# The tail of a two-layer transformer kernel on one core: four engines' orders laid out anew

## What is computed

```python
x = x + attn(ln(x))      # 16 heads of 64, segments of 64 plus every 4th position within 256
x = x + ffn4(ln(x))      # FP4: gate, up (352 wide), silu(gate)*up, down, blocks of 16 quantised
x = x + mixer(ln(x))     # rms norm, q k v a g projections, scan over chunks of 64, gate,
                         # out projection, rms norm, silu MLP of 512
x = x + rwkv(ln(x))      # sigmoid(xr @ Wr) * (relu(xk @ Wk)^2 @ Wv), xr, xk mix x with x shifted by one
```

## Time and profile before

| | us |
|---|---|
| three runs, median | 478.84 |
| lowest, highest | 476.29, 480.12 |
| the profiled execution | 475.18 |
| its span (first to last instruction) | 473.2 |
| TensorE busy in the span | 446.8 |

### The profile page before, as it was taken

The page is one execution under the profiler, slowest core; times in us unless marked ns, Lnnn a source line. Parts: engine busy times, 40 slices in busy tenths (PEclk is TensorE's granted clock), DMA queues, the critical chain, the costliest instruction groups (busy, mean ns, idle before and its releaser), DMA issues.

```text
span 473.2 us, 17264 instructions
## 1 busy us (share of the span) xinstructions
PE 446.8 (94%) x6440; PEld 350.3 (74%) x6440; DVE 395.1 (83%) x1344; ACT 332.3 (70%) x975; POOL 293.8 (62%) x491
## 2 busy tenths in 40 slices
PE   6899979999999999999999999999978889989995
PEld 5677768888888888788888888878644746558674
DVE  5987858888898899889899878987889988998674
ACT  3487747877877877886887786875655588986433
POOL 4234537677666858667867766737588896572122
PEclk9999989999999999999999999999999999999999
DMA  7369682346444444344456554443000000000002
GB/s 222 143 189 246 165 275 52 72 89 129 86 79 105 82 79 104 74 87 92 103 131 134 119 116 85 101 95 71 3 0 0 1 1 1 1 1 1 1 0 90
DMA packets 136098, 40.53 MB, mean 86 GB/s; under 512 B 104976, under 2 KB 131024, under 8 KB 136016
## 3 DMA queue, kind: packets, MB, share of 16 engines
q1 hardware_dynamic: 135440, 38.38, 35.3%
q10 hardware_dynamic: 576, 1.05, 0.7%
HBM read 29.44 MB, written 9.96 MB: 83 GB/s over the span
## 4 chain that ended last, share of the span: by engine, by line
PE 75%; POOL 8%; DVE 7%; ACT 3%; DMA 2%; issue 2%; SPq 1%; ACTq 0%; DVEq 0%; POOLq 0%
PE psum L423 13%; PE psum L465 12%; PE psum L485 7%; PE psum L499 6%; PE psum L1188 6%; PE psum L511 6%; PE psum L496 5%; PE psum L404 4%; PE psum L406 3%; PE psum L405 3%; PE psum L1183 3%; PE psum L1179 2%; POOL area L1834 2%; POOL rs L1879 1%; DMA arena<-in_L_attn_w_q_dram 1%
## 5 line engine op out<-in xcount | busy, mean ns | idle before, releaser
L949 POOL TENSOR_SCALAR pband<-pband,fac 128x192 f32<-128x192 f32 x256 | 103.9, 425 | 85.9 <-DVE fac L771 84.1
L569 ACT ACTIVATE pband<-pband,st 128x192 f32<-128x192 f32 x256 | 113.2, 448 | 0.2 <-DVE st L719 0.2
L719 DVE CUSTOM_DVE_ANT_0 pband<-psum,band_mask 128x192 f32<-128x192 f32 x256 | 76.0, 353 | 1.0 <-PE psum L423 0.9
L423 PE MATMUL psum<-keys,q_class 64*64 64x192 f32 (+2 forms) x1536 | 66.2, 275 | 0.0
L465 PEld LDWEIGHTS psum<-ident,pband 128*128 128x128 f32 x384 | 45.3, 141 | 21.2 <-issue 12.6
L423 PEld LDWEIGHTS psum<-keys,q_class 64*64 64x64 f32 x1536 | 57.4, 133 | 2.8 <-issue 2.0
L465 PE MATMUL psum<-ident,pband 128*128 128x128 f32 x384 | 53.3, 274 | 2.4 <-DVE pt L780 2.4
L569 ACT ACTIVATION_READ_ACCUMULATOR pband<-pband,st 128x1 f32 x256 | 49.5, 193 | 0.0
L931 POOL COPY keys<-k_rows 128x512 f32<-128x512 f32 x32 | 36.1, 1127 | 17.2 <-issue 8.7
L780 DVE COPY pt<-psum 128x512 f32<-128x512 f32 x64 | 43.7, 683 | 3.0 <-PE psum L465 2.4
L939 POOL COPY q_class<-q_rows 128x512 f32<-128x512 f32 x32 | 36.1, 1129 | 11.1 <-ACT q_rows L609 11.1
(11 more groups left out here) (213 smaller groups left out, 1086.4 us busy)
## 6 DMA issues: line engine op xcount, KB each, us to landing
v_rows_dram<-arena SPq DMA_DIRECT2D x32, 256.0 KB, 3.2
v_both<-v_rows_dram SPq DMA_DIRECT2D x32, 256.0 KB, 3.7
v_seg<-v_rows_dram SPq DMA_DIRECT2D x64, 128.0 KB, 3.4
v_side<-v_rows_dram SPq DMA_DIRECT2D x96, 64.0 KB, 2.6
w_rows_dram<-st SPq DMA_DIRECT2D x64, 8.0 KB, 2.9
st<-w_rows_dram SPq DMA_DIRECT2D x64, 8.0 KB, 2.4
arena<-_attn_hidden_states_dram SPq DMA_DIRECT2D x4, 256.0 KB, 4.2
out_dram<-x SPq DMA_DIRECT2D x4, 256.0 KB, 2.5
```

What stands on the lines that cost most here:

```text
L423: return pe.matmul(bank[2 * r + head][rows, at:at + y.shape[1]], x, y, start=True, stop=True, skip_group_check=True)
L569: act.activation(x, x, ACT.Exp, bias=mine[:, head:head + 1], scale=-1.0, accum_out=mine[:, 2 + head:3 + head]).then_inc(s_exp, 1)
L719: dve.tensor_tensor_reduce(pband[:, G % P_SLOTS, c, head, :], bank[2 * r + head][:, at:at + BAND], band_mask[:, (0, 1, 1, 2)[w], SEG * (1 ...
L949: pool.tensor_scalar(x, x, fac[:, F % 2, 1, c, head:head + 1], 1.0, ALU.mult, ALU.mult).then_inc(s_scaled, 1)
```

## The change

The same steps, each on the engine where it was, stand in another order in the lists of TensorE, ScalarE, VectorE and GpSimd, and `STEPS` says so. SyncE's list and all helper functions are unchanged. From the middle of the file on each line number is one smaller in the new file. Cut to the parts that are spoken of below:

```diff
@@ -543,19 +543,20 @@
-            weigh(28, 2); weigh(28, 3); turn(29, 1); turn(29, 0); output(28); turn_weights(0); turn_weights(1); t1(0)
-            turn(29, 3); turn_weights(2); turn(29, 2); weigh(29, 0); weigh(29, 1); turn_weights(3); turn_weights(4)
-            turn_weights(5); turn_weights(6); turn(30, 0); weigh(29, 2); weigh(29, 3); turn(30, 1); turn(30, 2)
-            turn_weights(7); output(29); turn(30, 3); weigh(30, 0); weigh(30, 1); t1(1); weigh(30, 2); weigh(30, 3)
-            turn(31, 0); turn(31, 1); output(30); turn(31, 3); turn(31, 2); weigh(31, 0); t2(0); weigh(31, 1); t1(2)
-            gu0(0); weigh(31, 2); weigh(31, 3); output(31); gu1(0); t1(3); t2(1); gu2(0); gu0(1); gu1(1); gu3(0)
-            gu2(1); t2(2); gu0(2); gu3(1); gu1(2); t2(3); gu2(2); gu0(3); gu3(2); gu1(3); t3a(0); t3b(0); gu2(3)
-            dn(0); t3a(1); gu3(3); t3b(1); dn(1); t4(0); pv(0); pk(0); pg(0); pa(0); pq(0); t3a(2); qq(0); t3b(2)
-            t4(1); dn(2); t3a(3); pk(1); t3b(3); pv(1); dn(3); pa(1); pg(1); t4(2); trx(0); pq(1); pk(2); pv(2); qq(1)
...
+            weigh(28, 2); weigh(28, 3); turn(29, 1); turn(29, 0); output(28); turn_weights(0); turn(29, 3)
+            turn_weights(1); turn_weights(2); t1(0); turn_weights(3); turn(29, 2); turn_weights(4); weigh(29, 0)
+            weigh(29, 1); turn_weights(5); turn_weights(6); turn_weights(7); turn(30, 0); weigh(29, 2); weigh(29, 3)
+            turn(30, 1); turn(30, 2); output(29); turn(30, 3); weigh(30, 0); weigh(30, 1); t1(1); weigh(30, 2)
+            weigh(30, 3); turn(31, 0); turn(31, 1); output(30); turn(31, 3); t2(0); turn(31, 2); weigh(31, 0); gu0(0)
+            t1(2); weigh(31, 1); weigh(31, 2); weigh(31, 3); gu1(0); output(31); t2(1); t1(3); gu2(0); gu0(1); gu3(0)
+            gu1(1); t2(2); gu2(1); gu0(2); gu1(2); t2(3); gu3(1); gu0(3); gu2(2); t3a(0); gu1(3); t3b(0); gu3(2)
+            dn(0); gu2(3); t3a(1); t3b(1); gu3(3); dn(1); t4(0); pv(0); pk(0); t3a(2); pg(0); t3b(2); pa(0); pq(0)
+            t4(1); dn(2); qq(0); t3a(3); pv(1); t3b(3); pk(1); pg(1); dn(3); pa(1); t4(2); pq(1); trx(0); qq(1)
+            pv(2); pk(2); pg(2); t4(3); op(0); trx(1); pv(3); pa(2); pk(3); pq(2); pg(3); pa(3); op(1); qq(2); pq(3)
...
@@ -680,19 +681,19 @@
-            take_out(28); odd_turned(29, 1); band_exps(31, 1); exp_difference(30); take_weights(0); take_weights(1)
-            odd_turned(29, 3); take_weights(2); take_weights(3); take_weights(4); z0(0); take_out(29)
-            odd_turned(30, 1); take_weights(5); exp_difference(31); take_weights(6); take_weights(7)
-            odd_turned(30, 3); qx6(0); take_out(30); odd_turned(31, 1); odd_turned(31, 3); z0(1); silu0(0)
...
+            take_out(28); odd_turned(29, 1); band_exps(31, 1); take_weights(0); exp_difference(30); take_weights(1)
+            take_weights(2); take_weights(3); take_weights(4); odd_turned(29, 3); take_weights(5); take_weights(6)
+            z0(0); take_weights(7); take_out(29); odd_turned(30, 1); exp_difference(31); qx6(0); odd_turned(30, 3)
+            take_out(30); odd_turned(31, 1); odd_turned(31, 3); z0(1); silu0(0); qx6(1); take_out(31); silu1(0)
...
@@ -899,25 +900,24 @@
...
-            bn0(1); qx7(0); ag0(1); even_turned(31, 0); qx8(0); xq(0); even_turned(31, 2); accumulate(30); xqt(0)
-            qx0(1); x1(2); qx2(1); bn0(2); ag0(2); hm0(0); qx7(1); accumulate(31); qx8(1); qx0(2)
-            x1(3); hm1(0); qx2(2); bn0(3); ag0(3); qa0(0); hm2(0); hm0(1); qa2(0); qx7(2); qx8(2); qx0(3)
-            hm1(1); qa0(1); qx2(3); hm3(0); qb0(0); hm2(1); qb2(0); qa2(1); qx7(3); hm0(2); qx8(3)
-            qa7(0); hm3(1); qb0(1); hm1(2); qa8(0); qb2(1); qb7(0); hm2(2); qb8(0); hm0(3); qa0(2)
-            qa7(1); qa2(2); qa8(1); hm1(3); qb7(1); hm3(2); qb8(1); qb0(2); qa0(3); hm2(3); qb2(2); x2(0)
-            bn1(0); ag1(0); qa2(3); hm3(3); qb0(3); qa7(2); qa8(2); qb7(2); qb2(3); x2(1)
-            qb8(2); bn1(1); ag1(1); qa7(3); a1(0); qa8(3); h1(1); qb7(3); qb8(3); aa(0); hqb(3); rq(0)
-            x2(2); bn1(2); e1(0); p(0); ag1(2); f(0); w(0); s(0); x2(3); bn1(3); ag1(3); a1(1); aa(1); qn(0); m(0)
-            w(1); v(2); p(1); h1t(3); rq(1); e1(1); x3_(0); f(1); w(2); qn(1); s(1); m(1); a1(2); y(1); aa(2); h2(0)
-            a1(3); x3_(1); h2t(0); rq(2); aa(3); e1(2); p(2); rq(3); f(2); qn(2); s(2); m(2); e1(3); qn(3); p(3)
...
+            even_turned(30, 2); qx7(0); x1(1); qx8(0); bn0(1); ag0(1); even_turned(31, 0); xq(0); xqt(0)
+            even_turned(31, 2); accumulate(30); qx0(1); qx2(1); x1(2); hm0(0); bn0(2); ag0(2); qx7(1); qx8(1); hm1(0)
+            accumulate(31); qa0(0); qx0(2); x1(3); qx2(2); bn0(3); hm2(0); ag0(3); qa2(0); qx7(2); hm0(1); qx8(2)
+            hm3(0); qb0(0); qx0(3); hm1(1); qx2(3); qb2(0); qa0(1); qa7(0); qx7(3); qx8(3); hm0(2); hm2(1); qa8(0)
+            qa2(1); qb7(0); hm1(2); qb8(0); hm3(1); qb0(1); hm0(3); qb2(1); qa7(1); qa0(2); hm2(2); qa8(1); hm1(3)
+            qb7(1); qa2(2); qb8(1); hm3(2); qa0(3); qb0(2); x2(0); qb2(2); bn1(0); hm2(3); ag1(0); qa7(2); qa2(3)
+            qa8(2); qb7(2); hm3(3); qb8(2); x2(1); qb0(3); bn1(1); ag1(1); qb2(3); qa7(3); h1(1); qa8(3); qb7(3)
+            qb8(3); a1(0); hqb(3); aa(0); w(0); x2(2); bn1(2); ag1(2); rq(0); p(0); e1(0); f(0); s(0); w(1); x2(3)
+            bn1(3); a1(1); ag1(3); qn(0); aa(1); m(0); v(2); rq(1); p(1); h1t(3); e1(1); f(1); qn(1); x3_(0); s(1)
...
@@ -1008,12 +1008,11 @@
-            rs0(1); qx1(1); qx4(1); rs0(2); xq(1); qx1(2); qx4(2); rs0(3); qa1(0); shift_weights(); 
-            qa4(0); qx1(3); xq(2); qa1(1); qx4(3); qb1(0); qb4(0); xq(3); qa4(1); qb1(1)
-            hqa(0); qb4(1); hqb(0); qa1(2); hqa(1); qa4(2); hqb(1); qb1(2); qa1(3); qb4(2)
-            rs1(0); qa4(3); rz1(0); qb1(3); hqa(2); qb4(3); hqb(2); rs1(1); rz1(1); hqa(3); rx(0); u(0)
...
+            rs0(1); qx1(1); qx4(1); shift_weights(); rs0(2); xq(1); qa1(0); qx1(2); qx4(2); rs0(3); qa4(0); xq(2)
+            qx1(3); qb1(0); qx4(3); qb4(0); xq(3); qa1(1); hqa(0); qa4(1); hqb(0); qb1(1); qb4(1); qa1(2); hqa(1)
+            qa4(2); hqb(1); qb1(2); qa1(3); qb4(2); rs1(0); hqa(2); qa4(3); hqb(2); qb1(3); rs1(1); qb4(3); rz1(0)
+            hqa(3); rz1(1); u(0); rs1(2); rx(0); u(1); rs1(3); y(0); rx(1); rz1(3); u(2); rs3(0); rz1(2); rx(2)
...
@@ -1021,36 +1020,36 @@
-        "t1 t2 gu0 gu1 gu2 gu3 t3a t3b dn t4 pv pk pg pa pq qq trx op t5 fc0 fc1 fc2 fc3 pr t6 k r kv",
+        "t1 t2 gu0 gu1 gu2 gu3 t3a t3b dn t4 pv pk pg pa pq qq trx op t5 fc1 fc0 fc3 fc2 pr t6 k r kv",
...
```

62 lines of the change are left out of this document (31 added, 31 removed), and 24 rows, old and new, of the table STEPS.

## The result

The changed kernel took 471.78 us (median of 4 runs, 470.72 to 472.09) beside 477.56 for the kernel before; the ratio of the runs is 0.987, 95% interval 0.984 to 0.991. Run again among the experiments, on another chip, it took 474.09 us (7 runs, 470.69 to 475.74) beside 477.62: 0.992, 0.988 to 0.995. So it is faster, by 1.3% in the one measurement and by 0.8% in the other: 472.1 us over its eleven runs, against 476.9 to 477.6 for before beside it and beside the experiments. The forecast was 475.8 us, 0.6% less than before: right in sign, too small by half against the first measurement. Both medians lie in its range; the first is faster by over 1%, which had a chance of 27%, the second within 1%, which had 69%.

A forecast was written before the change was run, and what follows sets the result against it. TensorE, busy 94% of the span, and its holes (13.1 us idle in the tail) set the time. Gains 0.4 + 1.2 + 0.3 + 0.5 + 1.5 = 3.9, less 0.9, give 3.0 us: 475.8 us, range 471.5 to 480.5.

The forecast's parts named there:

- the last 45 us: From 423.2 us TensorE never stops: no wait becomes real there, and a microsecond won earlier moves the end by one.
- C: Rival, slower: TensorE's queue is held at t3a(2) waiting for hqb(2), 2.4 us lost; 481.3 us, chance 9%.
- 318 to 329.4: Tail stretch in us: factors(31) and its accumulation come earlier, shrinking t1(1)'s wait of 0.55; gain 0.4 us.
- 329.4 to 353.6: Tail stretch: output(31)'s hole closes, gu1(1)'s shrinks, t2(1)'s grows to 1.3; gain 1.2 us.
- 353.6 to 369.7: Tail stretch: four old holes go, new waits of 1.2 at gu1(2) and 1.3 at t2(2); gain 0.3 us.
- 369.7 to 379.7: Tail stretch: waits before dn(1) and t4(0) go, a new 0.6 before t3b(1); gain 0.5 us.
- rival B: The VectorE and GpSimd chain swallows the gain, TensorE merely waiting longer at later steps; 478.3 us, chance 22%.
- 379.7 to 401: Tail stretch: t3a(2) fills the 0.72 wait for v(0), t4(2)'s 1.17 goes, 1.3 stays; gain 1.5 us.
- 401 to 423.2: Tail stretch: old waits of 2.15 us replaced by new ones at t4(3), qq(3) and trx(3); gain 0.
- behind it there is only the last output's two VectorE steps and the store, the same before and after: After 468.2 us, the end of TensorE's work: 5.0 us, taken as unchanged.
- I charge 0.9: Deduction of 0.9 us for VectorE operations on two SBUF tiles meeting GpSimd multiplications and blocking each other.
- rival A: Leads are kept and VectorE-GpSimd meetings get fewer: 3.9 + half of 3.4 = 5.6 us, 473.2 us; chance 27%.

The follow-up runs named there:

- h2: The changed kernel's four lists up to 370 us, the lists of the kernel before behind that: 478.39 us, ratio to before 1.003.
- e1: The changed kernel with VectorE's differences(31) put back behind qx1(0), where it stood before: 471.95 us, ratio to before 0.988.
- e5: The changed kernel with e1's edit and qa0(1) moved behind qa7(0) on VectorE: 472.04 us, ratio to before 0.989.
- e6: The changed kernel with e1's edit, gu3(1) put ahead of gu1(2) on TensorE, hm2(1) and silu3(1) moved earlier: 471.69 us, ratio to before 0.989.
- e4: The changed kernel with t3a(2) back behind pq(0), t3b(2) behind t4(1), and their ScalarE copies later: 476.09 us, ratio to before 0.997.
- b2: The kernel before with b1's edits and z2(0) moved behind ht2(2) on ScalarE: 481.6 us, ratio to before 1.010.
- h3: The lists of the kernel before up to 401 us, the changed kernel's behind that: 475.04 us, ratio to before 0.995.
- e2: The changed kernel up to 451.6 us, the last orders of the kernel before behind that: 475.37 us, ratio to before 0.992.
- b1: The kernel before with only the changed kernel's GpSimd piece, and qb8(2) behind qb7(2) on VectorE: 488.8 us, ratio to before 1.025.
- h1: The lists of the kernel before up to steps begun by 369.7 us, the changed kernel's behind: 472.01 us, ratio to before 0.989.
- e3: The changed kernel with GpSimd's piece put back as before, qa4(3), rz1(0), qb1(3) ahead of hqa(2): 478.24 us, ratio to before 0.999.

## Why the prediction was right and wrong

**Right.** The sign; that no hole appears in the last 45 us and that a lead is passed on (3.7 us at op(2), 3.5 at the end); that output(31) and v(0) no longer hold TensorE; the waits at t2(2), t3b(1) and pv(0), to 0.1 us; that C would not come: hqb(2) ended at 381.36, 1.1 us ahead of pk(0)'s end, where I had it 1 us ahead.

**Wrong: "318 to 329.4 ... Gain 0.4", "329.4 to 353.6 ... gain 1.2", "353.6 to 369.7 ... gain 0.3", "369.7 to 379.7 ... gain 0.5".** 2.4 us in all, and pv(0) came at the same time (0.1 us later). h2 shows it without the rest: this half of the change is worth nothing. The step that failed first is 318 to 329.4: I followed exp_difference(31) and factors(31) and not differences(31), which the change moves ahead of qx0(0) and where VectorE then stands 2.55 us for a DMA. The gain of 0.4 became a loss of 0.5 in the first profile and of 0.1 in the middle one of seven; e1, e5 and e6 put the price of the step at about 0.7. The second is gu1(2), sized 1.2 and measured at 2.78. I took silu, product and hand-overs, as if VectorE were free; but hm0(2) stands behind qa7(0), met by qb4(0) (2.11 us), qx7(3) and qx8(3). The third is t4(0): its wait for h1(0) did not go but grew from 0.46 to 0.67 us. The holes I closed came back at the next step that needs the chain: rival B's reasoning, true for this half.

**Wrong in size: "379.7 to 401 ... gain 1.5".** This is the term that was furthest off for what it gained: 3.4 us, from pv(0) to t4(2). The "about 0.5 behind t3a(3)" that I had set against it did not come, so that of the old 2.82 us of idle time only pv(0)'s 0.78 stayed: 2.0. The other 1.3 us the idle times don't show; part of them is that work begun behind a wait reads longer, the rest I have not split. And the reason beside it, "filled by t3a(2)", was wrong (e4, b2): ScalarE's z2(0) went out of the way, and I had not looked at ScalarE's list there.

**Off by little: "401 to 423.2 ... Gain 0".** The lead of 3.2 us at t4(2) is 3.7 at op(2) and 3.5 at the end, 0.3 more. I had put new waits of 0.95 at t4(3) and 0.6 each at qq(3) and trx(3) against the old 2.15; they were 0.51, 0.25 and none, with 0.25 before qq(1) that I didn't have. h3, which has these orders alone, is 0.6 us ahead at op(2) and 0.4 at the end.

**Wrong: "behind it there is only the last output's two VectorE steps and the store, the same before and after".** The stores of other groups share the end. 0.9 us: 6.98 to 7.01 against 6.08 to 6.14 in all profiles (e2).

**Wrong in sign: "I charge 0.9" for meetings.** They fell by 1.9 us where I charged for more; rival A had "half of 3.4" = 1.7. How much of that reached TensorE can't be told apart: b1 and b2 had the long ones gone as well and won nothing.

Together, by the profiles: -0.14 + 3.36 + 0.29 + 0.89 = 4.4 us (up to pv(0), to t4(2), to TensorE's end, behind it), where I had 2.4 + 1.5 + 0 + 0 less 0.9 = 3.0. The terms up to pv(0) were 2.5 too high and those behind it 3.0 too low. That these two nearly cancel is luck; what is left of the miss is them and the 0.9 charged for meetings. The outcome is nearest to rival A's, the leads kept and fewer meetings, though not by its way; its 473.2 us lies between the two measurements' 471.8 and 474.1.

Open: why the first comparison gives 5.8 us and the tails 4.4. The profile of before was one of its quicker executions (475.18 us, median 477.4 over 75), and the two measurements of the changed kernel differ by 2.3 us, at mean clocks of 0.9955 and 0.9921; I can't do better than 0.8 to 1.3%. Open too is each engine's share. No kernel I ran beats the changed one by more than the measurement can tell (h1, e1, e5 and e6 took 471.7 to 472.0).

## What to carry to other kernels

When a hand-written order of several engines is changed, follow for each moved step what it waits for, DMAs included, and what stands behind it on its own engine; the steps that decided here (differences(31), z2(0), rz1(0)) were small ones on engines that I had looked at only for the big ones. A hole closed on TensorE alone, ahead of a saturated chain, came back here at the chain's next delivery (h2); where VectorE was ahead too, the lead was kept (e1). And what a step behind a DMA costs is seen only over several profiles. Count what leaves at the end, all stores of it, not the last alone.

## What the runs showed of the hardware

A long wait of TensorE may cost twice: behind the wait of 2.2 to 2.8 us before gu1(2) the granted clock fell to 0.5, from 2.4 to 1.2 GHz, for 3.4 us or twice that in six profiles of nine, 1.7 us of clock for each 3.4, and in none of seven without that wait. That they hang together is likely, not proven: six of these seven have the old order there, and e6 alone changed the wait and little else. It fell elsewhere too behind two shorter waits in a row, 0.88 and 0.78 us (h1, at 381.5) and 0.83 and 0.98 (e4, at 393.1), and in one of 2.21 and one of 3.37 us (e3, at 333.5 and 391.5); behind the pair before t4(0) and pv(0), which all sixteen profiles have, only in h1.

The long waits of one order came out the same in every profile (t2(1) 1.79 to 1.80 us, gu1(2) 2.77 to 2.78), but for those on a DMA (t1(1), 0.61 to 2.21); the stretches at the lower clock did not come in every one, so a single profile is no measure of an order's time.
